# A one-head graph layer that also normalizes and routes its nodes, and expert rows written to their node's place

## The reference, cut to what matters

```python
x1 = jax.nn.elu(_gat(x, src, dst, W1, ..., heads=8, concat=True))
x2 = jax.nn.elu(_gat(x1, src, dst, W2, a_src2, a_dst2, b2, heads=1, concat=False))
...
x = x + x2
xn = _layernorm(x)                                    # first norm
xn = (xn - mu) * lax.rsqrt(var + EPS) * gamma + beta  # second norm, of the normed rows
logits = xn @ Wr + br                                 # 8 experts
top_vals, top_idx = jax.lax.top_k(logits, 2)
w = jax.nn.softmax(top_vals, axis=-1)
y_e = gelu(xn @ W1[e] + b1[e]) @ W2[e] + b2[e]        # for the two chosen e
x = x + sum(w_e * y_e)
```

## Time and profile before

| | |
|---|---|
| median of 3 runs | 4164.31 us (4163.76 to 4167.91) |
| the profiled execution, its own time | 4165.42 us |
| its span, first to last instruction | 4163.6 us |
| mean granted TensorE clock | 0.893 |
| PE busy | 3143.5 us (75%) |
| DVE busy | 2956.5 us (71%) |
| ACT busy | 2282.2 us (55%) |
| POOL busy | 161.9 us (4%) |

### The profile page before, as it was taken

How to read it: one execution, slowest core, us unless ns; L and a number is a source line. 1 busy time by engine, 2 the same in 40 slices (tenths; PEclk the granted TensorE clock), 3 DMA queues, 4 the chain that set the end, 5 groups by cost and what they waited for, 6 DMA issues and landing times. The chain is left out here.

```text
span 4163.6 us, 46261 instructions
## 1 busy us (share of the span) xinstructions
PE 3143.5 (75%) x15892; PEld 1616.9 (39%) x15893; DVE 2956.5 (71%) x3388; ACT 2282.2 (55%) x3191; POOL 161.9 (4%) x150
## 2 busy tenths in 40 slices
PE   3024766888888875998399459999999999679587
PEld 2012333322222223887367243333333332367454
DVE  4878986899999994443634339999999999621423
ACT  2000367899999994011033118898989899322022
POOL 0000000000000000010022400000000000000000
PEclk8556998999999997999599779999999999889599
DMA  1000234333333331431422222222222222200000
GB/s 44 0 0 10 79 141 164 107 95 96 97 95 96 95 95 53 175 126 63 143 63 64 75 95 74 77 76 76 75 78 75 78 76 78 85 22 0 10 6 31
DMA packets 180360, 311.08 MB, mean 75 GB/s; under 512 B 26768, under 2 KB 131070, under 8 KB 179672
## 3 DMA queue, kind: packets, MB, share of 16 engines
q1 hardware_dynamic: 175048, 294.76, 22.9%
q0 software_dynamic: 5136, 14.03, 1.2%
HBM read 247.26 MB, written 61.47 MB: 74 GB/s over the span
## 5 line engine op out<-in xcount | busy, mean ns | idle before, releaser
L891 PE MATMUL acc<-weights,messages 128*64 128x400 f32 x3200 | 622.3, 516 | 151.1 <-DVE weights L959 89.1
L1912 PE MATMUL acc<-weights,values 128*64 128x400 f32 x3200 | 639.5, 521 | 13.5 <-DVE weights L2022 9.3
L2019 DVE SCALAR_TENSOR_TENSOR weights<-x,counts 128x1600 f32<-128x1600 f32 x304 | 555.0, 1826 | 33.1 <-ACT x L1988 25.0
L1899 PE MATMUL scores<-q,k 32*128 32x400 f32 x3200 | 390.1, 557 | 70.2 <-ACT x L1983 64.0
L891 PEld LDWEIGHTS acc<-weights,messages 128*64 128x64 f32 x3200 | 202.4, 138 | 567.5 <-DVE weights L959 194.6
L1985 ACT ACTIVATE x<-scores 128x800 f32<-128x800 f32 x496 | 404.7, 838 | 17.1 <-PE scores L1899 17.1
L959 DVE SCALAR_TENSOR_TENSOR weights<-rho,kappa,counts 128x800 f32<-128x800 f32 x400 | 410.6, 1068 | 2.0 <-PE acc L891 2.0
L964 DVE TENSOR_TENSOR weights<-maxima,counts 128x1600 f32<-128x1600 f32 x200 | 364.1, 1821 | 42.8 <-ACT maxima L916 42.8
L911 ACT ACTIVATE maxima<-rho,wx 128x800 f32<-128x800 f32 x400 | 361.9, 952 | 34.7 <-DVE weights L964 30.3
L916 ACT ACTIVATE maxima<-maxima,kappa 128x800 f32<-128x800 f32 x400 | 360.2, 948 | 0.0
L1912 PEld LDWEIGHTS acc<-weights,values 128*64 128x64 f32 x3200 | 196.6, 137 | 407.5 <-issue 253.9
(11 more groups left out here) (293 smaller groups left out, 3678.0 us busy)
## 6 DMA issues: line engine op xcount, KB each, us to landing
counts<-edge_counts SPq DMA_DIRECT2D x200, 400.0 KB, 3.1
counts<-edge_counts SPq DMA_DIRECT2D x400, 200.0 KB, 2.4
edge_counts<-counts_out SPq DMA_DIRECT2D x40, 1000.0 KB, 4.2
counts<-edge_counts SPq DMA_DIRECT2D x25, 1600.0 KB, 6.6
expert_rows<-t SPq DMA_DIRECT2D x57, 128.0 KB, 1.7
w_first<-in_L_ffn_W_dram SPq DMA_DIRECT2D x8, 512.0 KB, 9.5
w_second<-in_L_ffn_W_dram SPq DMA_DIRECT2D x8, 512.0 KB, 8.9
normed_rows<-t SPq DMA_DIRECT2D x1, 3200.0 KB, 11.5
```

Source lines behind the costliest of these rows:

```text
L891: ins = nc.tensor.matmul(acc[64 * o:64 * o + 64, p, h, 0:CH], msg[:, t, r % 2 * Q + q, :], w[:, T % WR, q, half(h)], start=(t == 0), stop= ...
L1899: ins = nc.tensor.matmul(sc[:, (n + j // 2) % SR, j % 2, 0:CH], kT[part, r % KF, t * P:(t + 1) * P], q[part, r % 2, :], start=True, stop=True)
L1912: ins = nc.tensor.matmul(acc[64 * e:64 * e + 64, p, 0:CH], msg[:, t, r % KF * 2 + p, D * e:D * e + 2 * D], w[:, U % WR, 2 * p + e, :], sta ...
L2019: ins = nc.vector.scalar_tensor_tensor(out=w[:, U % WR, :, :], in0=out, scalar=EXP_HI, in1=counts, op0=ALU.min, op1=ALU.mult)
```

## The change

The one-head stage now carries each chunk on to its router values while the next chunk's matmuls run, and the experts' rows are stored at their node's place. In the one-head stage the chunk loop is written out; `rho` has two buffers; between the weights of source tiles t DVE does parts of the chunk before: the sums after t = 4, elu and addition after 7, statistics after 9, the normed rows after 11, router bias after 21, the two greatest after 22, their indices after 23. ACT does elu, root and the evacuation of the flipped rows; POOL has no work there. TensorE flips the chunk before in three groups ahead of t = 8, 10 and 12 and makes its logits ahead of t = 14. The two norms become one, with the variance v replaced by v(1+eps)+eps², which is what norming twice gives. The row of a sixth chunk is no longer made. SP stores the normed rows chunk by chunk, and loads the counts ahead of the bias row. `stage_norm` ahead of the experts and the router at the head of `stage_experts` are gone.

```diff
+        rho = core.sb(ctx, "rho", [P, 2, 2, TH])
...
+        def flip_group(pe, i, n):
+            pe.wait_ge(s_norm, i * TC + (TC if n == 2 else 4))
+            if n == 0 and i:
+                pe.wait_ge(s_logit, i)
+            if n and i < NTC:
+                pe.wait_ge(s_exp, min(i + 2, NTC))
...
+        def logits(pe, i):
+            pe.wait_ge(s_xt, (i + 1) * EVACS)
...
+                    ins = nc.tensor.matmul(flip[:, t * NE:(t + 1) * NE], XT[:, k, at:at + P], wr[:, k, :],
...
+        def elu_exp(act, i):
+            for d in range(TC):
+                act.wait_ge(s_raw, i * TC + d + 1)
+                nc.scalar.activation(ey[:, d, :], y[:, d, :], ACT.Relu, scale=-1.0).then_inc(s_relu, 1)
+            for d in range(TC):
+                act.wait_ge(s_relu, i * TC + d + 1)
+                nc.scalar.activation(ey[:, d, :], ey[:, d, :], ACT.Exp, scale=-1.0).then_inc(s_ey, 1)
...
+                for i in range(NTC):
                     for t in range(NT):
+                        if i and FLIP_AT <= t < FLIP_AT + 6 and (t - FLIP_AT) % 2 == 0:
+                            flip_group(pe, i - 1, (t - FLIP_AT) // 2)
+                        if i and t == ROUTE_AT:
+                            logits(pe, i - 1)
...
+                        for d in range(TC):
+                            if i and t == 0:
+                                pe.wait_ge(s_raw, (i - 1) * TC + d + 1)
```

```diff
+                sp.wait_ge(s_down, TILES)
                 for u in range(YR):
                     sp.wait_ge(s_st[u], (TILES - u + YR - 1) // YR * 16)
+                for n in range(NL):
+                    for j in range(2):
+                        first_row = SPARE + j * NP + n * ST * P
+                        sp.dma_start(chosen_rows[j][:, n * ST:(n + 1) * ST, :],
+                                     rows_out[first_row:first_row + ST * P, :].rearrange("(t p) f -> p t f", p=P)).then_inc(s_yg[n], 16)
...
+                for j in range(GX):
+                    gather(j)
+                pool.wait_ge(s_node, 2)
+                for j in range(TILES):
+                    pool.wait_ge(s_y, j + 1)
+                    nc.gpsimd.indirect_dma_start(out=rows_out[:, :], out_offset=bass.IndirectOffsetOnAxis(home[:, j:j + 1], 0),
+                                                 in_=yb[:, j % YR, :], in_offset=None).then_inc(s_st[j % YR], 16)
+                    if j + GX < TILES:
+                        pool.wait_ge(s_flip, j + 1)
+                        gather(j + GX)
...
+                link(nc.vector.tensor_scalar(part[:, 2, :], part[:, 1, :], float(-SPARE), 0.0, ALU.add, ALU.max))
+                link(nc.vector.tensor_scalar(part[:, 3, :], part[:, 2, :], float(NP), float(-NP), ALU.is_ge, ALU.mult))
+                nc.vector.tensor_tensor(node[:, :], part[:, 2, :], part[:, 3, :], ALU.add).then_inc(s_node, 1)
```

More of the change, by code:

```diff
@@ L1016, in make_row @@
+        banks = (flip, row[:, 0, :], row[:, 1, :])
+        EVACS = 4
+        def make_row(i):
             for h in range(2):
                 for k in range(KF):
-                    ins = nc.tensor.matmul(row[:, h, 0:TH], wdb[:, k, 0, :], XT[:, k, bass.ds(first + h * TH, TH)],
+                    ins = nc.tensor.matmul(row[:, h, 0:TH], wdb[:, k, 0, :], XT[:, k, i * TN + h * TH:i * TN + (h + 1) * TH],
                                            start=(k == 0), stop=(k == KF - 1))
             ins.then_inc(s_row, 1)
-        def make_rho():
-            nc.scalar.activation(rho[:, :, :], row[:, :, 0:TH], ACT.Exp, bias=bias[:, 0:1], scale=-0.8).then_inc(s_exp, 1)
@@ new lines, in root, with turn_rows @@
+        def root(act, i):
+            act.wait_ge(s_var, i + 1)
+            nc.scalar.activation(std[:, :], std[:, :], ACT.Sqrt).then_inc(s_std, 1)
+        def turn_rows(act, i):
+            act.wait_ge(s_rt, 64)
+            for n in range(3):
+                act.wait_ge(s_flip, i * 3 + n + 1)
+                for k, j, t, m in ((n, 0, 0, 4),) if n < 2 else ((0, 0, 4, 1), (1, 1, 4, 1)):
+                    at = (i * TC + t) * P
+                    nc.scalar.activation(XT[:, k, at:at + m * P], banks[n][:, j * P:(j + m) * P], ACT.Identity,
+                                         scale=gb[:, 0, k:k + 1], bias=gb[:, 1, k:k + 1]).then_inc(s_xt, 1)
@@ new lines, in add_elu @@
+        def add_elu(dve, i):
+            for d in range(TC):
+                dve.wait_ge(s_ey, i * TC + d + 1)
+                nc.vector.scalar_tensor_tensor(out=y[:, d, :], in0=y[:, d, :], scalar=0.0, in1=ey[:, d, :],
+                                               op0=ALU.max, op1=ALU.add).then_inc(s_elu, 1)
+            for d in range(TC):
+                dve.wait_ge(s_elu, i * TC + d + 1)
+                node = X[:, i * TC + d, :]
+                nc.vector.scalar_tensor_tensor(out=node, in0=y[:, d, :], scalar=-1.0, in1=node, op0=ALU.add, op1=ALU.add
+                                               ).then_inc(s_x, 1)
@@ new lines, in norm @@
+        def norm(dve, i):
+            dve.wait_ge(s_std, i + 1)
+            nc.vector.reciprocal(std[:, :], std[:, :]).then_inc(s_scale, 1)
+            if i:
+                dve.wait_ge(s_store, i * 16)
+                dve.wait_ge(s_flip, i * 3)
+            dve.wait_ge(s_scale, i + 1)
+            for d in range(TC):
+                nc.vector.tensor_scalar(normed[:, d, :], X[:, i * TC + d, :], mv[:, d, 0:1], std[:, d:d + 1],
+                                        ALU.subtract, ALU.mult).then_inc(s_norm, 1)
@@ L1076, in _ @@
[L1076 to L1087 removed]
+                make_rho(act, 0)
@@ L1089, in _ @@
+                for i in range(NTC):
+                    if i:
+                        elu_exp(act, i - 1)
+                        root(act, i - 1)
+                        turn_rows(act, i - 1)
+                    if i + 1 < NTC:
+                        make_rho(act, i + 1)
+                elu_exp(act, NTC - 1)
+                root(act, NTC - 1)
+                turn_rows(act, NTC - 1)
             @block.vector
             def _(dve):
-                nc.vector.sem_inc(s_raw, 1)
-                dve.wait_ge(s_b, 16)
@@ L1117, in stage_gat_one_head @@
+                last = NTC - 1
+                read_sums(dve, last)
+                add_elu(dve, last)
+                variance(dve, last)
+                norm(dve, last)
+                add_bias(dve, last)
+                top(dve, last)
+                index(dve, last)
+                dve.wait_ge(s_index, NT)
     core.stage_ends()
@@ L1404, in stage_experts @@
     HM = HID // P
-    S2, GX, GY, YR = 2 * NT, 6, 8, 3
+    S2, GX, YR = 2 * NT, 6, 4
+    SPARE = TILES * P
     I32 = mybir.dt.int32
```

315 lines of the change are left out of this document (174 added, 141 removed).

## The result

The changed kernel takes **4060.72 us** (median of 4 runs, 4059.45 to 4063.81), the kernel before beside it 4166.11 (4163.76 to 4167.95): a ratio of **0.9748, 95% interval 0.9732 to 0.9765**. The forecast was 4065 in a range of 4053 to 4088. The profiled execution has a span of 4057.7 us against 4163.6, 105.9 less; the sum had 99.2. That the two are near each other is partly luck: one term gave 10 us more than counted and another 12 less.

A forecast was written before the change was run, and what follows sets the result against it. The prediction took serial work outside the loops, which another engine could hide, as the bound. Terms -31.4 - 28.5 + 0 - 33.1 - 6.2 = -99.2 us against the median 4164.3 gave 4065 us, range 4053 to 4088.

The forecast's parts named there:

- The boundaries: One-head stage, four chunk ends: TensorE waits 0.8 us in place of 3.17, -9.5 us.
- Flips and router matmuls: One-head stage: ten flips and ten router matmuls added on TensorE for four chunks, +12.8 us, and +1.6 of wait.
- Rival 2: One-head stage: the hidden work isn't hidden, DVE late to the norms, and the gap stays; 4091 us, half 4078; chance 0.12.
- the term of +2.5: One-head stage: TensorE's last matmul moves by +2.5 us in sum, from 1969.3 to 1971.8.
- The tail: Last chunk of the one-head stage, without cover: serial steps to the indices 22.6 us, then change of stage 0.5.
- The experts' head: Start of the experts' stage: first use of the indices after 1.4 us in place of 31.16; -28.5 us in all.
- The loop: Expert loop: POOL's added store per tile fits in the 4.10 us pace; 0, bounds 0 and +15 us.
- Rival 4: Expert loop: POOL becomes the bound through slow stores; 4188 us at 5 us for store and issue; chance 0.03.
- The sum: Sum over experts: reads in order, then 50 additions of 0.485 us without waits, ending at 2368.7, not 2401.8; -33.1 us.
- The gap: Behind the last addition: the 6.80 us before the next stage shrink as POOL's last indirect DMA comes earlier; -6.2 us.
- Rival 1: Behind the sum over experts: the gap before the next stage stays; 4071 us; chance 0.27.
- rival 3: Sum over experts: the transfers at the end are slow, as scattered rows; 4098 us; chance 0.05.

The follow-up runs named there:

- The run with the fillers: The changed kernel with each chunk's sums read before the next chunk's first weight tile, and seven unused matmuls filling TensorE's idle time there: 4065.88 us.
- the one-IOTA run: The changed kernel with one added small GpSimd IOTA at the start of the one-head stage: 4050.14 us.
- 14-gather run: The changed kernel with 14 GpSimd indirect gathers that nobody reads, issued one behind the other during the sum over experts: 4073.35 us.

## Why the prediction was right, and where its terms were not

*The boundaries* (-9.5 counted) gave -15.6, the term that was too small. The idle time fell from 3.17 to 0.97, as forecast (0.8): -8.8. What I left out is TensorE's clock: the slices of 0.50 behind each boundary were in the trace of before, and their loss of 1.7 us each (slices of 2 us at 0.78, 0.50 and 0.87 lose 0.44 + 1.00 + 0.26), another -6.8, went with the idle time. The run with the fillers shows it apart from the idle time: 63.2 us a chunk and not 64.9.

*Counts ahead of the bias row* (-0.3) is -2.4 to -2.6: I took the price of the issue for the price of the order.

*Flips and router matmuls* (+12.8 and +1.6 of wait): a chunk's work apart from its idle time is 60.88 - 0.97 = 59.9 us. In the kernel before the period was 61.5; without 3.17 of idle time and 1.7 of slow clock 56.6 are left. So the addition is 3.3 a chunk, 13.2 in all, against 14.4; there was no wait at the flips, since the norms were done 17.0 us after the chunk's end, where I had counted 18.4 for the fourth. Rival 2 is out. Together (-2.1, +0.7, -6.8, -1.2) that is -9.4 of the -9.9 by which the term of +2.5 was off.

*The tail* (22.6 and 0.5 of change of stage) was 22.4 in all. The Trainium skill (ScalarE: Activation LUTs, What ACT_TABLE_LOAD costs) would add a drain of 1.38 to the load of 1.28. The row shows the load beginning 0.02 us after the last relu's end and the first exp 0.01 after the load: no drain is visible here.

*The experts' head* (-28.5) failed by 12 us. The step that failed is "the 31.16 us up to the first use of the indices become 1.4, five small constants of POOL at about 0.2". It was 12.2, since GpSimd runs the first of them 11.1 us after its configuration change: +10.8. The first flip came 8.3 us behind the first gather, where 6.5 were counted (+1.8; that gather landed late, after 8.2 us, and why was not tried), and the steps from the indices to the gather took 0.7 less. The trace of the kernel before had rows that told of the wait, and the prediction doesn't use them: the 7.0 us ahead of its first IOTA, and the configuration change of the one-head stage at 1654.6, ahead of the first multiplication on GpSimd (a MEMSET had run at 1654.37 without a wait). By moving that multiplication and the addition off GpSimd the change moved the configuration change onto the path, and the one-IOTA run took it off again.

*The loop* (0): the pace is 4.10 before and after, and where the stretch's -2.3 comes from was not traced. The scatter is as cheap as the gather it stands beside (all of the changed kernel; min, median and max in ns):

```profile
L1684 POOL DMA_INDIRECT expert_rows<-t,place_of_row x57: 958/977/1003, 2047.1 to 2277.2; - x57
...
DMA to landing us min/median/max: 2.4/2.4/4.4
```

Rival 4 is out. Whether the DVE copies that the prediction names here would slow GpSimd's issues, these rows can't tell: each DVE instruction of this loop reads a result of TensorE (`up`, `down`, `hidden_flip`), and none copies from SBUF to SBUF.

*The sum* (-33.1) was -36.2. The additions go at 0.40 us each (20.1 for 50; each overlaps the next), not 0.485: -4.1. The first comes 10.65 us behind the last tile's addition instead of 9.7, +0.9: the last scatter is issued 1.7 us behind it instead of 0.1, SP's first read follows 2.5 us later where 3.7 were counted, and the rows are there after 6.5 us instead of 5.9.

*The gap* (-6.2) was -6.5, for the reason given, a queue of GpSimd that is done long before; the "9 us after POOL's last indirect DMA" in it was no fixed cost: it grows with the burst. Rival 1 is out, as is rival 3: the reads ran at some 348 GB/s.

## What to carry to other kernels

When work is moved off an engine, list what that engine did first in each stage: a one-time cost that was hidden can land on the path. On GpSimd a pair of MODIFY_POOL_CONFIG rows in the queue warns of it, and it was in the trace of the kernel before. Not each pair costs: behind the first one, at 1.2 us of that kernel, the next instruction ran at once (1.26). A gap in TensorE's work costs more than its own length if the clock falls behind it, so look at the granted clock in 2 us slices behind each gap, and compare a gap of 1 us with one of 3. And price a reorder of transfers by when the waited-for one lands, not by the issue of the one moved.

## What was not expected of the hardware

- Behind a reduction over partitions GpSimd changes its configuration ahead of its next IOTA (in the one-head stage of the kernel before, ahead of a TENSOR_TENSOR), and the IOTA comes 7.0 to 11.4 us after the change (11.1 in the changed kernel, 11.85 us of DVE's wait). A MEMSET in between doesn't bring it forward. That the reduction is the cause was not tried.
- 3.2 us without matmuls: clock 0.50 for about 3 us behind. 0.97 us: none of it.
- The next stage begins 3.7 us after the issue of a last indirect gather has ended, its landing within them, and 0.08 later for each further one in the burst.
- Gathers issued beside the reads and additions of the sum took up to 5.64 us (14-gather run) where undisturbed ones take 0.95. Which of the two neighbours does it was not tried.
